# Spline layer spread over the cross steps, sums of the third normalization behind the rows of step 38, no unread matmuls in the fifth lead step

## What is computed

```python
x = _layernorm(x + attention1(x))
x = _layernorm(x + self_attention(x) + cross_attention(x, ctx))
# routed feed-forward: tile_idx picks one of 64 experts for each token
h = gelu(xf @ compress_w1 + compress_b1)
comp = tanh(h @ compress_w2 + compress_b2)                       # 2 numbers a token
hh = relu(einsum('ni,nig->ng', comp, spline_w1[tile_idx]) + spline_b1[tile_idx])
mag = einsum('ng,ngo->no', hh, spline_w2[tile_idx]) + spline_b2[tile_idx]
y = xf + mag * directions[tile_idx] * output_scale[0]
y = normalize(y) * norm_gamma + norm_beta
x = _layernorm(x + y)
```

## Time and profile before

| what | us |
|---|---|
| median of 3 runs | 2227.47 (2224.45 to 2228.35) |
| the profiled execution | 2221.05 |
| its span, first to last instruction | 2219.3 |
| PE busy | 2093.4 (94%) |
| DVE busy | 1754.5 (79%) |
| ACT busy | 1533.8 (69%) |
| POOL busy | 755.5 (34%) |

### The profile page before, as it was taken

The page is one execution under the profiler, slowest core; times in us unless marked ns, Lnnn a source line. Parts: engine busy times, 40 slices in busy tenths (PEclk is TensorE's granted clock), DMA queues, the critical chain, the costliest instruction groups (busy, mean ns, idle before and its releaser), DMA issues.

```text
span 2219.3 us, 39450 instructions
## 1 busy us (share of the span) xinstructions
PE 2093.4 (94%) x13138; PEld 911.5 (41%) x13138; DVE 1754.5 (79%) x4869; ACT 1533.8 (69%) x3361; POOL 755.5 (34%) x802
## 2 busy tenths in 40 slices
PE   5999999999999999999999999999999999989983
PEld 2344334543444434543335433454344533444332
DVE  6957779688987889778897788968888787977754
ACT  2936887478865888458894688747886578846861
POOL 3026521165113650155402653116521353004620
PEclk8899999999999999999999999999999999999995
DMA  3700034000520006100160003400043000610000
GB/s 111 138 10 1 1 67 86 11 2 1 114 49 10 2 20 124 20 11 2 39 124 10 1 1 76 87 11 1 1 96 58 11 1 11 113 30 1 1 11 10
DMA packets 250858, 81.80 MB, mean 37 GB/s; under 512 B 236064, under 2 KB 247328, under 8 KB 250656
## 3 DMA queue, kind: packets, MB, share of 16 engines
q1 hardware_dynamic: 250656, 79.29, 17.6%
HBM read 16.35 MB, written 4.19 MB: 9 GB/s over the span
## 4 chain that ended last, share of the span: by engine, by line
PE 76%; DVE 12%; ACT 8%; issue 3%; DMA 1%; SPq 0%; POOL 0%; DVEq 0%; POOLq 0%; ACTq 0%
PE bank L1738 14%; PE bank L1807 14%; PE bank L1798 10%; PE bank L1421 7%; PE bank L1734 6%; ACT work L772 5%; PE bank L1795 4%; PE bank L1691 4%; DVE work L977 3%; PE bank L1554 3%; PE bank L1541 2%; PE bank L1577 2%; PE bank L1848 2%; PE bank L1767 1%; DVE stats L982 1%
## 5 line engine op out<-in xcount | busy, mean ns | idle before, releaser
L831 ACT ACTIVATE work<-bank 128x512 f32<-128x512 f32 (+3 forms) x1536 | 723.0, 549 | 261.9 <-PE bank L1795 140.5
L1244 DVE TENSOR_REDUCE top_half<-bank 128x1 f32<-128x512 f32 x1024 | 636.4, 683 | 139.7 <-PE bank L1738 138.4
L1738 PE MATMUL bank<-k_c,q_c 32*128 32x512 f32 x2048 | 536.0, 618 | 0.0
L1798 PE MATMUL bank<-q_c,k_c 32*128 32x512 f32 x2048 | 467.4, 624 | 7.4 <-DVE q_c L1270 6.0
L772 ACT ACTIVATE work<-work,neg 128x512 bf16<-128x512 bf16 x512 | 362.7, 716 | 30.6 <-DVE work L977 29.8
L1807 PE MATMUL bank<-work,v_flat 128*32 128x512 f32 (+3 forms) x3072 | 365.0, 551 | 0.6 <-ACT work L831 0.3
L977 DVE TENSOR_SCALAR_CACHE_REDUCE work<-bank 128x512 bf16<-128x512 f32 x512 | 322.3, 685 | 35.2 <-PE bank L1523 25.1
L1241 DVE CUSTOM_DVE_ANT_0 masked<-bank,mask_w 128x384 bf16<-128x384 f32 (+3 forms) x512 | 226.6, 489 | 118.5 <-PE bank L1734 113.9
L654 POOL TENSOR_TENSOR featA<-featA,featB 128x512 f32<-128x512 f32 (+3 forms) x232 | 241.9, 1043 | 225.9 <-ACT featB L844 223.0
L1738 PEld LDWEIGHTS bank<-k_c,q_c 32*128 32x128 f32 x2048 | 210.9, 183 | 159.8 <-DVE top_half L1244 125.7
L615 POOL TENSOR_SCALAR ln_r<-mv 128x4 f32<-128x4 f32 x32 | 9.0, 281 | 748.9 <-DVE mv L986 748.9
(11 more groups left out here) (208 smaller groups left out, 2627.6 us busy)
## 6 DMA issues: line engine op xcount, KB each, us to landing
xT_pad<-xT SPq DMA_DIRECT2D x16, 256.0 KB, 2.9
ctx_sb<-ctxT SPq DMA_DIRECT2D x8, 512.0 KB, 3.4
x_res<-x SPq DMA_DIRECT2D x8, 512.0 KB, 5.0
out<-r_sb SPq DMA_DIRECT2D x8, 512.0 KB, 2.9
work<-work SPq DMA_TRANSPOSE x112, 4.5
qk_sb<-qkT SPq DMA_DIRECT2D x1, 512.0 KB, 4.6
pe_sb<-pe_w SPq DMA_DIRECT2D x1, 256.0 KB, 4.0
v_sb<-vT SPq DMA_DIRECT2D x1, 256.0 KB, 5.0
```

Source lines behind the costliest of these rows:

```text
L831: nc.scalar.activation(pT[:, s % PT_SLOTS, g, q0:S], exp_bank(n)[:, 0:S - q0], ACT.Exp, scale=SCALE).then_inc(pT_ready, 1)
L1244: nc.vector.tensor_reduce(top_half[:, i % 2, g, u // 2, u % 2:u % 2 + 1], scores, AX.X, ALU.max, negate=True).then_inc(slot_out, 1)
L1738: mm(dst, q_c[rows, i, P * t:P * (t + 1)], k_c[rows, i, S * half:S * (half + 1)], start=True, stop=True, tile_position=(GW * g, 0)).then_i ...
L1798: mm(dst, k_c[rows, i, P * u:P * (u + 1)], q_c[rows, i, :], start=True, stop=True, tile_position=(GW * g, 0)).then_inc(sT_mm, 1)
```

## The change

Three things change.

First, ACT copies what the gather made out of PSUM (`gathered`, behind the evacuation of `unit(3)`): the parameters into `params_sb`, which shares the widened `sig_raw`, the directions into `xs_flat`, which is `z_sb`. `unit(4)` waits for the first copy, `unit(5)` and the last value tiles for the second (`gather_out`). The spline reads the copies.

Second, the spline's thirteen operations are cut into eight parts, one in each of the steps 18 to 25, between the second and the third maximum of the step. In the tail they stand behind each other as before, behind both copies.

Third, the eight unread matmuls of the fifth lead step are gone, and `third_sums` stands behind `put_rows` in step 38.

```diff
-    EXPERT_LEAD, GATHER_LEAD, SPLINE_LEAD = 1, 2, 3
+    EXPERT_LEAD, GATHER_LEAD = 1, 2
+    SPLINE_PARTS, SPLINE_FROM = 8, 18
...
+            def gathered(c):
+
+                params, *dirs = GATHER_BANKS
+                act.wait_ge(gather_in, c + 1)
+                nc.scalar.copy(params_sb, bank[:, params, 0:NT * PARAMS]).then_inc(gather_out, 1)
+                nc.scalar.copy(xs_flat, bank[:, dirs[0]:dirs[-1] + 1, :].rearrange("p a n -> p (a n)")).then_inc(gather_out, 1)
...
-                units(3, 4, 5)
+                units(3)
+                if prev:
+                    gathered(c)
+                units(4, 5)
...
-            def spline(c, sf):
+            def spline(c, sf, part):
...
-                param = bank[:, GATHER_BANKS[0], 0:NT * PARAMS].rearrange("p (t n) -> p t n", t=NT)
+                param = params_sb.rearrange("p (t n) -> p t n", t=NT)
...
+                if part == 0:
+                    dve.wait_ge(comp_done, c + 1)
+                    dve.wait_ge(gather_out, 2 * c + 2)
+                    sf.mark(nc.vector.tensor_tensor(hh, param[:, :, w1:w1 + G], column(0), ALU.mult))
+                    do(nc.vector.tensor_tensor(hh2, param[:, :, w1 + G:b1], column(1), ALU.mult))
+                if part == 1:
+                    do(nc.vector.tensor_tensor(hh, hh, hh2, ALU.add))
+                    do(nc.vector.tensor_tensor(hh, param[:, :, b1:w2], hh, ALU.add))
+                if part == 2:
+                    do(nc.vector.tensor_scalar(hh, hh, 0.0, None, ALU.max))
+                    do(nc.vector.tensor_tensor(hh, param[:, :, w2:b2], hh, ALU.mult))
+                if part == 3:
+                    do(nc.vector.tensor_reduce(mag, hh, AX.X, ALU.add))
+                    do(nc.vector.tensor_tensor(mag, param[:, :, b2], mag, ALU.add))
+                    do(nc.vector.tensor_scalar(mag, mag, scale_col[:, 0:1], None, ALU.mult))
+                if part >= SPLINE_PARTS - NT:
+                    t = part - (SPLINE_PARTS - NT)
+                    made = nc.vector.scalar_tensor_tensor(z_sb[:, t, :], z_sb[:, t, :], mag[:, t:t + 1], r_sb[:, t, :], ALU.mult, ALU.add)
...
-                    if prev and m == SPLINE_LEAD:
-                        spline(c, sf)
                 for s in range(ALL_STEPS):
-                    if prev and s == LATE_STEP:
-                        third_sums(c, sf)
...
+                    if prev and 0 <= s - SPLINE_FROM < SPLINE_PARTS:
+                        spline(c, sf, s - SPLINE_FROM)
                     for tile in behind_tiles:
                         maximum(*tile)
...
+                    if prev and s == LATE_STEP:
+                        third_sums(c, sf)
...
                     if prev and u == 4:
-                        pe.wait_ge(param_read, b)
+                        pe.wait_ge(gather_out, 2 * b - 1)
                     if prev and u == 5:
-                        pe.wait_ge(spline_done, b)
+                        pe.wait_ge(gather_out, 2 * b)
...
-                    if prev and m == 4:
-                        pe.wait_ge(pj_evac, b * 2 * UNITS + 8)
-                        keep_clock(7, FILLERS)
```

More of the change, by code:

```diff
@@ L116, in decoder_layer @@
     DVE_STEPS = 5
-    FFN_STEPS = 70
+    FFN_STEPS = 71
     SIG_STEPS = 29
@@ L137, in decoder_layer @@
         bcq_col, bck_col = sb("bcq_col", [P, HG]), sb("bck_col", [P, HG])
-        one_col, live_col = sb("one_col", [P, 2]), sb("live_col", [P, 2])
+        half_cols = sb("half_cols", [P, 2, 2])
+        one_col, live_col = half_cols[:, 0, :], half_cols[:, 1, :]
         bv_row, bcv_row, bp_row = sb("bv_row", [P, D]), sb("bcv_row", [P, D]), sb("bp_row", [P, D])
         gamma_row, beta_row = sb("gamma_row", [P, D]), sb("beta_row", [P, D])
-        sig_raw = sb("sig_raw", [P, D])
+        sig_wide = sb("sig_wide", [P, NT * PARAMS])
+        sig_raw = sig_wide[:, 0:D]
         sig_work = sb("sig_work", [TILES, 2, D])
@@ L239, in decoder_layer @@
         tile_scores = sig_raw[:].rearrange("p (t n) -> p t n", t=NT)
+        params_sb = sig_wide[:]
         hT = sig_work[:].rearrange("p a d -> p (a d)")
@@ L279, in decoder_layer @@
         expert_ready, tiles_in = sem("expert_ready"), sem("tiles_in")
-        gather_in, param_read, spline_done = sem("gather_in"), sem("param_read"), sem("spline_done")
+        gather_in, gather_out, spline_done = sem("gather_in"), sem("gather_out"), sem("spline_done")
         out_dma = sem("out_dma")
@@ L1112, in spline @@
[L1112 to L1118, removed]
@@ L1119, in spline @@
-                dve.wait_ge(param_read, c + 1)
-                do(nc.vector.tensor_scalar(mag, mag, scale_col[:, 0:1], None, ALU.mult))
-                for t in range(NT):
-                    made = nc.vector.scalar_tensor_tensor(z_sb[:, t, :], bank[:, GATHER_BANKS[1 + t // 2], D * (t % 2):D * (t % 2 + 1)],
-                                                          mag[:, t:t + 1], r_sb[:, t, :], ALU.mult, ALU.add)
+                if part == 0:
[3 more added lines that the diff above has]
+                    do(nc.vector.tensor_tensor(hh2, param[:, :, w1 + G:b1], column(1), ALU.mult))
@@ L1124, in spline @@
+                if part >= SPLINE_PARTS - NT:
+                    t = part - (SPLINE_PARTS - NT)
+                    made = nc.vector.scalar_tensor_tensor(z_sb[:, t, :], z_sb[:, t, :], mag[:, t:t + 1], r_sb[:, t, :], ALU.mult, ALU.add)
                     if t == NT - 1:
                         made.then_inc(spline_done, 1)
+                        sf.wait(dve)
+                        dve.wait_ge(spline_done, c + 1)
                     else:
                         sf.mark(made)
-                sf.wait(dve)
@@ L1129, in spline @@
-                dve.wait_ge(spline_done, c + 1)
             def third_sums(c, sf):
@@ L1347, in tail @@
                 expert_columns(base, tail_uses)
-                spline(c, sf)
+                for part in range(SPLINE_PARTS):
+                    spline(c, sf, part)
                 third_sums(c, sf)
```

3 lines of the change are left out of this document (removed).

## The result

The changed kernel takes 2239.34 us, median of 4 runs (2236.99 to 2241.16), where the kernel before took 2227.39 in runs beside it (2224.45 to 2228.35): a ratio of 1.0056, 95% interval 1.004 to 1.0072. It is 12 us slower. The forecast was slower by 18.6, and the time lies in the forecast range. The profiled execution spans 2236.8 (2238.55 in all), against 2219.3 before: 17.5 more.

What follows compares the result with a forecast made beforehand. PE bounds the kernel (76% of the span), so only its waits count. -18.6 + 24.5 + 11.3 + 1.4 = +18.6 on 2221.05 gives 2239.65; with the median 6.4 above that execution, forecast 2246.1, range 2230 to 2252.

Steps and rivals of the forecast that it cites:

- Lead: Lead steps: unread matmuls and the wait for DVE go, two ACT copies come; -2.65 a batch, -18.6 over 7 batches.
- leave the clock alone: Fifth lead step: the fifth unit replaces the unread matmuls at once, so PE stays as busy; clock left in the remainder.
- Pieces: Steps 18 to 25: spline pieces delay the fourth maximum and PE's second half, two wait for POOL; 3.5 a batch, +24.5.
- step 18: First spline piece, between the second and third maximum: makes the fourth maximum late; 0.44 a batch.
- Step 23: Cross step whose piece meets POOL's addition of 755.80 to 757.07: 0.35 bare, 0.7 more for the wait.
- the 2.25: Batch 0: DVE's addition of two SBUF tiles, 1.18 elsewhere, took 2.25 beside POOL's; read as waiting for POOL's end.
- Rival (b): Cross steps: DVE's idle 0.44 are room, so the pieces cost nothing; -5.9, 2221.6 us; chance 0.10.
- Rival (a): Cross steps: the pieces meet POOL's additions and do not wait; +6.1, 2233.6 us; chance 0.17.
- with step 23's wait alone: Variant of the POOL rival: only the piece in step 23 waits; +10.8, 2238.3 us; chance 0.15.
- Sums behind rows: Step 38: PE's 0.85 wait goes, but burst 9's output addition comes late; 1.8 a batch, +11.3 in all.
- rival (c): Steps 38 to 42: burst 9 does not hold PE, its slot is free in time; +7.3, 2234.8 us; chance 0.09.
- Tail: End of the kernel: the spline now waits for both ACT copies, 0.39 + 1.01; +1.4, once.

Runs made afterwards that it cites:

- the filled kernel: The kernel before with the third norm's sums behind step 38's row addition, plus ten unread matmuls in front of step 40's weighted values; 2257.46 us, ratio 1.0137.
- Part 3 alone: The kernel before with only the third norm's sums moved behind the row addition in step 38; 2250.35 us, ratio 1.0094; again 2243.72, ratio 1.0076.
- the other parts: The changed kernel with `third_sums` back at its old place in front of step 38's work; 2217.98 us, ratio 0.9961; again 2222.10, ratio 0.9974.
- the kernels with the pieces elsewhere: The changed kernel with sums in front, pieces behind the fourth maximum: 2210.82 us; with pieces where VectorE stands idle, sums cut in two: 2206.44 us.

## Why the prediction was right, and where it was off

**Lead: right.** -2.65 a batch forecast, -2.77 measured, the scores at 0.71 as taken. The unread matmuls filled a wait, as the prediction reads it. That their going would leave the clock alone, because the fifth unit takes their place at once, is not so in every batch: that unit took 3.42 in the batches 4 and 6, in both executions of the changed kernel, and the two cost 3.0.

**Pieces: the mechanism right, the size off.** +3.5 a batch forecast, +2.69 measured; over seven batches this is 5.7 of the sum. By the copies behind each step, in all seven batches alike to 0.03: step 18 +0.23 (0.44 forecast), 20 +0.32 (0.40), 21 +1.13 (1.23), 22 +0.07 (0), 23 +0.49 (1.05), 25 +0.40 (0.35), and -0.02 to 0.03 in the others. Step 23 is the term that was mis-sized: the row update met GpSimd's addition, but it lasted 0.89 in place of 0.47, not 1.1. It ended 0.28 behind GpSimd's, so some 0.19 of its own time seems to have run during the wait, and of its 0.89 in front of the fourth maximum 0.49 were paid. The prediction's own row had a sign of this: it read the 2.25 as waiting to the hundredth, but GpSimd's end at 281.04 and 1.18 behind it make 282.22, and the addition ended at 282.13. Step 18 had 0.2 of slack that the prediction did not give it. That most of the price is of the place is shown: +0.69 behind the fourth maximum. Rival (b) is false as it was put, for the place that the change chose, and true one place on: the 0.44 are room, but behind the fourth maximum. Rival (a) is false: both pieces wait, the 128x4 addition to the hundredth. (Its sum is +6.0, and with step 23's wait alone +10.9, each 0.1 off in the prediction.)

**Sums behind rows: right at full clock, and one thing left out.** +1.8 a batch forecast, +1.78 measured, and the wait where it was put; rival (c) is false. The output addition stands 9.56 behind the row addition, 4.71 + 4.80 = 9.51 by the sum. Left out was the clock: the prediction considered it at the removed matmuls only, not behind the wait that it had itself forecast. There it fell in four of six batches, in the filled kernel in none.

**Tail: right**, +1.4 forecast and 1.39 from the copies' start to the spline; 0.7 of it is left at the end, since a later wait of 0.17 went and the tail before varies by some tenths.

**The sum.** +18.6 forecast, +11.1 at full clock: 5.7 of the difference is the pieces. In the median it is +12. The forecast stands 7 above the measured time.

**Luck in the total.** The medians do not add up by the full-clock terms. Part 3 alone gives +23 and +17 where its term is +11.5 (forecast +11.3), and the other parts give -9.4 and -4.3 for -0.4 (forecast +7.3). Each pair sums to +13 or +14, about the +12 of the whole. So the forecast of the whole is only 7 off because one half came out 6 to 12 above its forecast and the other 12 to 17 below it.

By the granted clocks most of this is the clock. Every execution has its time and its mean granted clock on record: the 21 executions with the other parts average 0.973, the 59 of the kernel before, run beside the experiments, 0.969. Among executions of one clock, from 0.969 to 0.972, ten with the other parts and 38 of the kernel before differ by 0.1 at most in the mean; part 3 alone stands 12.6 to 13.9 above the kernel before at its clock, and the changed kernel 11.7 to 12.7. These are the full-clock terms within some 2.5. The measure is rough: the kernel that only lacks the unread matmuls stands 1 to 5 below the kernel before by it.

**What stays open** is why the clock falls less with the other parts. In the traces with them (12.49 and 34.07) the excess outside the stretches behind burst 9 is 3.2, 5.1, 5.3 and once 9.4, against 8.3 before and 11.4 and 8.1 with part 3 alone, but the kernels with the pieces elsewhere have 11 to 12. No run tells the cause.

## What to carry to other kernels

Idle time of an engine has a place in its loop. Here work in front of the operation that frees the next buffer cost 2.69 a batch, and the same work behind it 0.69, so look for which of the four operations the other engine waits. Swapping two pieces of work on an engine that is busy from one handover to the next only moves the wait to the later handover. And a wait made for the matmul engine is priced with what runs behind it: here a wait that costs 1.78 at full clock brought up to 2.9 more at a lower one.

## What the runs showed of the hardware

- A small VectorE operation from SBUF to SBUF, started while GpSimd adds two SBUF tiles, ends 0.01 to 0.04 behind GpSimd's end (1.12 and 1.27 for one of 0.16). With one input it is the same (0.68). The maxima, which read PSUM, go on beside such an addition: the four of step 21 take 2.48.
- Not every GpSimd operation holds VectorE. Beside its power operation (2.93) a small one takes 0.15 to 0.17, and beside its multiplication of one tile (819.51 to 821.08) VectorE's addition of two SBUF tiles, begun at 820.47, takes 1.18, as elsewhere.
- The Trainium skill (GPSIMD Engine Reference, section Key points) names VectorE's instructions with two SBUF inputs, and those in a two-port mode, as the ones that meet GpSimd. The first half agrees with the 1.12, but not with the 0.15 to 0.17 of the two-input addition beside the power operation. Whether the multiplication with one input belongs to the second half no row here can show.
- The same wait of 2.63 of TensorE lowers the granted clock in some batches and not in others, and executions of one kernel agree on which: 1, 2, 3 and 5 in both of the changed kernel, 1, 2, 3, 5 and 6 in both with part 3 alone. In the changed kernel the two that are spared, 4 and 6, are those whose fifth unit took 3.42; whether the one has to do with the other is not shown. It costs 1.4 to 2.9 each time.
- Batch 0's start varies from 128.7 to 135.0 between executions of kernels that are alike up to there: a single profiled execution is no measure of a few us.
